# Third convolution: nine-tap products in f32r with stacked high and low parts, weights split in the stage

## The reference, cut to what matters

```python
def _L2_conv_ref(x, w_qkv, head_scale, w_out, gamma, beta):   # x comes in as _ln_c(x)
    ...
    qkv = lax.conv_general_dilated(x, w_qkv, (1, 1), 'SAME', ...)   # 3x3, 64 -> 384 channels
    q, k, v = jnp.split(qkv, 3, axis=1)                             # 8 heads of 16 each
    attn = jnp.einsum('bgnd,bgmd->bgnm', q, k)
    qn = jnp.sqrt(jnp.sum(q * q, axis=-1) + SMOOTH)
    kn = jnp.sqrt(jnp.sum(k * k, axis=-1) + SMOOTH)
    attn = attn / (qn[:, :, :, None] * kn[:, :, None, :] + SMOOTH)
    s = jax.nn.sigmoid(head_scale) * (0.4 - 0.003) + 0.003
    pb = jnp.exp(-(1.0 / (2.0 * s * s))[:, None, None] * dis[None, :, :])
    pb = pb / jnp.sum(pb, axis=-1, keepdims=True)
    out = jnp.einsum('bgnm,bgmd->bgnd', attn * pb[None], v)
    ...
```

## Time and profile before

| | us |
|---|---|
| median of 3 runs | 771.08 (768.73 to 773.09) |
| the profiled execution, its device time | 772.89 |
| its span, first to last instruction | 771.1 |
| the stage touched, first load to `sums(0)` of the attention | 358.70 to 411.42 |
| matmuls of line 1334 within it | 72 records, 36 in the program |

### The profile page before, as it was taken

How to read it: one execution, slowest core, us unless ns; L and a number is a source line. 1 busy time by engine, 2 the same in 40 slices (tenths; PEclk the granted TensorE clock), 3 DMA queues, 4 the chain that set the end, 5 groups by cost and what they waited for, 6 DMA issues and landing times. The chain is left out here.

```text
span 771.1 us, 8274 instructions
## 1 busy us (share of the span) xinstructions
PE 589.8 (76%) x2469; PEld 353.7 (46%) x2469; DVE 501.7 (65%) x1226; ACT 377.9 (49%) x568; POOL 278.0 (36%) x219
## 2 busy tenths in 40 slices
PE   4663879999995698482997775599875997988781
PEld 2563657777773484261444442433533534751110
DVE  2772566777775653666954654882287893849986
ACT  3002647888873740252536652364023245939852
POOL 4998357788784100301005760500012382000000
PEclk9997689999997799576998557599579798569995
DMA  3441000000000500402000000300021000000000
GB/s 107 114 119 45 1 1 1 0 1 1 0 2 13 101 0 1 154 1 79 7 1 0 1 1 1 84 1 0 1 64 28 0 2 8 1 0 0 0 0 14
DMA packets 18516, 18.44 MB, mean 24 GB/s; under 512 B 10954, under 2 KB 14347, under 8 KB 18088
## 3 DMA queue, kind: packets, MB, share of 16 engines
q1 hardware_dynamic: 18472, 17.93, 8.9%
HBM read 17.02 MB, written 0.26 MB: 22 GB/s over the span
## 5 line engine op out<-in xcount | busy, mean ns | idle before, releaser
L646 POOL TENSOR_TENSOR l0f_hid_lo<-l0f_hid,l0f_hid_hi 114x512 fp32r<-114x512 f32 (+1 forms) x75 | 98.0, 1317 | 48.6 <-ACT l0f_hid_hi L728 47.8
L824 DVE TENSOR_TENSOR l0f_hid<-l0f_silu,PS 114x512 f32<-114x512 f32 x96 | 65.7, 687 | 41.8 <-ACT l0f_silu L745 40.7
L682 PE MATMUL PS<-l0f_xs,l0w_hi 128*114 128x512 f32 x192 | 78.6, 409 | 0.0
L682 PE MATMUL PS<-l0f_xs,l0w_lo 128*114 128x512 f32 x192 | 77.5, 403 | 0.0
L745 ACT ACTIVATE l0f_silu<-PS 114x512 f32<-114x512 f32 x96 | 57.7, 602 | 31.9 <-PE PS L682 31.2
L2530 PE MATMUL PS<-l3f_ring,l3f_slots 128*32 128x512 f32 x128 | 54.9, 647 | 13.0 <-DVE l3f_ring L2611 13.0
L728 ACT CAST l0f_hid_hi<-l0f_hid 114x512 fp32r<-114x512 f32 x96 | 59.1, 615 | 2.9 <-DVE l0f_hid L824 2.3
L1325 POOL TENSOR_TENSOR l2c_den<-l2c_far,l2c_den 128x1024 f32<-128x1024 f32 x16 | 37.6, 2358 | 63.2 <-ACT l2c_den L1483 63.2
L2611 DVE SCALAR_TENSOR_TENSOR l3f_ring<-l3f_ring,l_countT 128x1024 f32<-128x1024 f32 x32 | 39.0, 1226 | 10.4 <-ACT l3f_ring L2561 10.4
L2557 ACT ACTIVATE l3f_ring<-l3r_plain,l3r_neg 128x1024 f32<-128x1024 f32 x32 | 36.0, 1134 | 11.9 <-PE PS L2530 11.9
L2605 DVE SCALAR_TENSOR_TENSOR l3f_ring<-l3f_slope,l3r_low,l3f_ring 128x1024 f32<-128x1024 f32 x32 | 40.9, 1285 | 0.4 <-ACT l3f_ring L2557 0.4
(11 more groups left out here) (581 smaller groups left out, 1327.2 us busy)
## 6 DMA issues: line engine op xcount, KB each, us to landing
l0w_raw<-in_l_w SPq DMA_DIRECT2D x32, 170.5 KB, 3.2
l3k_edge<-in_edges SPq DMA_DIRECT2D x2, 1024.0 KB
l2c_wqkv<-in_l_wqkv SPq DMA_DIRECT2D x3, 384.0 KB, 4.3
l0w_w<-in_l_w SPq DMA_DIRECT2D x8, 142.5 KB
l2f_raw<-in_l_w SPq DMA_DIRECT2D x2, 512.0 KB, 6.2
l1c_pos_w<-in_l_pos_w SPq DMA_DIRECT2D x1, 784.0 KB, 4.7
l1c_vrow<-l1c_vimg SPq DMA_DIRECT2D x7, 88.0 KB, 4.0
l1f_raw<-in_l_w SPq DMA_DIRECT2D x2, 256.0 KB
```

The costliest lines, as they stand in the source:

```text
L646: g.tensor_tensor(hid_lo[0:k, q % HIDS, :], hid[0:k, q % HIDS, :], hid_hi[0:k, q % HIDS, :], ALU.subtract).then_inc(S("low_pool"), 1)
L682: last = t.matmul(m.PS[0:k, (one, two)[z], :], half[:, e, z, a:a + k], xs[:, h * HALF:(h + 1) * HALF], start=(half is ew.hi), stop=(half i ...
L824: v.tensor_tensor(hid[0:k, at % HIDS, :], silu[0:k, at % RING0, :], m.PS[0:k, two, :], ALU.mult).then_inc(S("free"), 1)
```

## The change

Images and weights are split into a high part, rounded to f32r, and a low part, the rest, also f32r. `xp` keeps its two halves, but they now hold the high part of the image (partitions 0 to 63, written by ACT) and the low part (64 to 127, DVE: bank of PSUM minus high part). The nine taps are no longer paired. One product for two images is 9 matmuls with 128 rows (high weights, standing in both halves, on both parts of the images) and 9 with 64 rows (low weights on the high part of the images), all f32r with 512 columns.

The weights come in f32 by 18 loads (6 per product: two copies of three rows of taps) of 64 partitions each, into `raw`, which lies in the tile `den`. ACT rounds them into `hi` (3 times 128 x 1152), and POOL subtracts into `lo` (3 times 64 x 1152), which lie in tiles that are used later. `xp` is zeroed by a POOL copy of a zeroed tile instead of a memset, since it is f32r. The copy of the transposed input to `XT` is left out. `q2` now shares the tile of `k2`.

```diff
         def _(sp):
             for z in (1, 0, 2):
-                sp.dma_start(wqkv[:, :, z, :], w["l2_wqkv"][:, :, z, :]).then_inc(S(f"w_conv{z}"), 16)
+                for half in range(2):
+                    for dy in range(3):
+                        src = w["l2_wqkv"][(dy % 2) * C:(dy % 2 + 1) * C, 3 * (dy // 2):3 * (dy // 2) + 3, z, :]
+                        sp.dma_start(raw[half * C:(half + 1) * C, z, 3 * dy:3 * dy + 3, :], src).then_inc(S(f"w_conv{z}"), 16)
             for dst, src in ((hs, "l2_hs"), (dis, "dis"), (parity, "parity")):
                 sp.dma_start(dst[:], w[src]).then_inc(S("w_first"), 16)
...
         @block.gpsimd
         def _(g_):
-            g_.memset(xp[:], 0.0).then_inc(m.sem("padded_zero"), 1)
+            g_.memset(blank[:], 0.0).then_inc(S("blank"), 1)
+            g_.wait_ge(S("blank"), 1)
+            g_.tensor_copy(xp[:].rearrange("p b h w -> p (b h w)"), blank[:, 0:1].broadcast_to([P, B * PADH * PADW])).then_inc(m.sem("padded_zero"), 1)
             g_.wait_ge(m.sem("padded_zero"), m.pads + 1)
             g_.memset(vt[:], 0.0).then_inc(S("vt_zero"), 1)
             g_.wait_ge(S("vt_zero"), 1)
+            for j, z in enumerate((1, 0, 2)):
+                g_.wait_ge(S("high"), j + 1)
+                g_.tensor_tensor(lo[z], raw[0:C, z], hi[0:C, z], ALU.subtract).then_inc(S("low"), 1)
...
             def conv(z, h, bank):
 
-                for j, (dy, dx) in enumerate(PAIRS):
-                    last = t.matmul(m.PS[:, bank, :], wqkv[:, j, z, :], xp[:, 2 * h:2 * h + 2, dy:dy + HH, dx:dx + WW],
-                                    start=(j == 0), stop=(j == len(PAIRS) - 1))
+                images = slice(2 * h, 2 * h + 2)
+                for j, (dy, dx) in enumerate(TAPS):
+                    t.matmul(m.PS[:, bank, :], hi[:, z, j, :], xp[:, images, dy:dy + HH, dx:dx + WW], start=(j == 0), stop=False)
+                t.wait_ge(S("low"), 1 + (1, 0, 2).index(z))
+                for j, (dy, dx) in enumerate(TAPS):
+                    last = t.matmul(m.PS[:, bank, :], lo[z][:, j, :], xp[0:C, images, dy:dy + HH, dx:dx + WW], start=False, stop=(j == len(TAPS) - 1))
...
         @block.scalar
         def _(a):
-            images_scalar(a, m, xp)
+            k = m.norms + 1
+            a.wait_ge(m.sem("norm_var"), k)
+            a.activation(m.stat[:, 2, :], m.stat[:, 1, :], ACT.Sqrt).then_inc(m.sem("norm_dev"), 1)
+
+            def round_high(z):
+                a.wait_ge(S(f"w_conv{z}"), 96)
+                a.copy(hi[:, z], raw[:, z]).then_inc(S("high"), 1)
+
+            a.wait_ge(m.sem("padded_zero"), m.pads + 1)
+            for b in range(B):
+                if b % 2 == 0:
+                    a.wait_ge(m.sem("norm_turned"), 2 * (k - 1) + b // 2 + 1)
+                a.copy(xp[0:C, b, 1:1 + HH, 1:1 + WW], turned(b)).then_inc(S("image_high"), 1)
+                if b == 1:
+                    round_high(1)
+            a.copy(m.XT[0:1, 0:1], m.ident[0:1, 0:1]).then_inc(m.sem("norm_xt"), 2)
+            round_high(0)
+            round_high(2)
             a.wait_ge(S("w_first"), 48)
             a.activation(hs[:], hs[:], ACT.Exp, scale=-1.0).then_inc(S("minus_exp"), 1)
...
-            images_vector(v, m, xp)
+            v.wait_ge(m.sem("padded_zero"), m.pads + 1)
+            for b in range(B):
+                v.wait_ge(S("image_high"), 2 * (b // 2) + 2)
+                v.tensor_tensor(xp[C:2 * C, b, 1:1 + HH, 1:1 + WW], turned(b), xp[0:C, b, 1:1 + HH, 1:1 + WW], ALU.subtract).then_inc(S("image_low"), 1)
```

27 lines of the change are left out of this document (17 added, 10 removed).

## The result

The changed kernel took 781.06 us in the median of 4 runs (778.91 to 781.37), the kernel before 770.05 in 4 runs beside it (768.73 to 773.09). The ratio is 1.013, with a 95% interval of 1.009 to 1.017: slower by 11 us. The forecast was 775.9, and the range ended at 780.5.

A forecast was written before the change was run, and what follows sets the result against it. In the third convolution TensorE ran without a hole, with a second chain (ACT, VectorE) 0.2 us behind. norm_rows(1) 7.9 us late, minus 3.1 from three products, gives +4.8: 772.89 + 4.8 - 1.81 = 775.9 us, range 771.3 to 780.5.

The forecast's parts named there:

- The delay of the chain: Third convolution: late loads, roundings and a POOL subtraction delay the exponential and first step on hs, hence pb, by 7.7 us.
- D: Lateness of the chain from hs through pb to the z sums and rz: 7.7 us, ends 6.5 and 8.6.
- The z sums: TensorE's z sums, behind idle time of 7 us or so, start at half clock and take 6.8 us instead of 4.5.
- The first product on the path: conv(0, 0), ahead of norm_rows(1): a product costs 4.1 us, and norm_rows(1) starts 7.9 us late.
- The gain of three products: Between norm_rows(1) and sums(0), three cheaper products give back 3 x 1.02 = 3.1 us.
- windows slow the stream: Rival: f32r matmuls on padded windows take 0.43 us (790) or 0.29 (780.0) instead of 0.23; chance 0.08.
- Bytes as the bound of the loads: Rival: bytes at 268 GB/s, not issue, pace the 18 loads; D 3.3 to 5.9, time 771.3 to 773.9; chance 0.2.
- A low clock through all of the z sums and beyond: Rival: TensorE's clock stays low past the z sums; its price is cut from the text, half lies outside the range.
- own range: 774.5 to 777.4 us, for D from 6.5 to 8.6 and the clock back after 3 to 6 us.
- the wide one: 771.3 to 780.5 us, from the low end of the byte-bound case to the smaller window case.

The follow-up runs named there:

- hs_first_fit: hs_first with POOL's subtraction for q moved behind the z sums and that for v behind VectorE's first split: 775.10 us, 3.7 above the kernel before.
- three_loads: The changed kernel with the weights laid out on the host and loaded by three 128-row loads instead of eighteen of 64 rows: 779.9 us.
- hs_first: The changed kernel with hs, dis and parity loaded behind the first six weight loads and the exponential of hs ahead of the second and third rounding: 779.4 us.
- combo: The changed kernel with three 128-row loads, sign loads and exponential moved ahead, and low weights of 128 rows: 776.58 us, 1.006 of the kernel before.
- combo_late: combo with POOL's second and third subtraction moved behind VectorE's eight far products: 778.0 us, 1.008 of the kernel before.
- late_hs: The kernel before with 15 idle 64-row loads put ahead of the loads of hs, dis and parity, products still paired f32: 1.010 of the kernel before.
- lo128: The changed kernel with low weights of 128 rows and no wait for them in the second product of each kind: 1.007 of the kernel before.
- fit: combo with POOL's subtraction for q moved behind the z sums and that for v behind VectorE's first split: 771.19 us against 771.43, ratio 1.0001.
- after: The changed kernel itself, as profiled: median 781.06 us, 1.013 of the kernel before.
- forms: The changed kernel with other operand forms in the q and v products and no low-weight wait in each second product; results not right, no time given.
- three_late: three_loads with POOL's second and third subtraction moved behind VectorE's eight far products: 781.3 us, 1.012 of the kernel before.
- combo64: combo with low weights of 64 rows again; no time given, sums(0) starts 3.6 us later than in combo.

## Why the prediction came out as it did

The direction and the mechanism were right: the loads are paced by SP, the roundings wait for them, the exponential waits for the roundings, POOL's third subtraction holds the first VectorE step, and the z sums start late and at half clock. The size was too small: +4.8 forecast for `sums(0)`, +10.1 measured there, and 11 in the time.

**The delay of the chain.** Forecast D = 7.7, measured 8.2 (17.65 - 9.44), within its ends. The loads went every 0.66 us instead of 0.61, which is 0.8 us over 17 of them (the prediction's own had this pace: three loads of 128 rows in 1.99 us, so the number of rows does not tell the pace, as it had taken); the shorter landing of 2.5 gave 0.4 back. The hold by POOL was as forecast: the step ended 0.04 us behind the subtraction.

**The z sums.** Forecast 6.8 us at half clock and back, measured 6.5; `norm_rows(0)` started at rel. 32.9, forecast 32.7. The k products were forecast to end by rel. 19.3 and ended near 22.7, since the clock stayed low for 12.7 us and not 3 to 6. So TensorE idled for 3.6 us ahead of the z sums where 7 or so were forecast. The later end cost nothing here, for `pb` was later still; in hs_first_fit, where `pb` ended at 20.65, the same late clock kept the z sums back until 22.67.

**The first product on the path.** Forecast `norm_rows(1)` at rel. 38.5, measured 39.6. conv(0, 0) took 5.3 us from its start to the next group's where 4.1 was forecast; the start of `norm_rows(0)`, 0.2 later than forecast, and the row sums' 0.3 less (1.4 instead of 1.7) make it 1.1. With the delay of the chain it makes `norm_rows(1)` late by 9.0.

**The gain of three products.** This is the step that failed most. The sum had 3 x 1.02 = 3.1 us back between `norm_rows(1)` and `sums(0)`; that way took 23.16 us instead of 22.07, so 1.1 was lost and the miss is 4.2. Where it went (the first three points make 2.5, the last 1.7):

- The value 0.23 for an f32r matmul on a window was wrong: it is 0.257. Over 18 matmuls that is 0.5 us a product. The rival "windows slow the stream" had the right mechanism and its smaller size, 0.29, was too high.
- The change of rows between the halves was in no part of the prediction, which so put it at nothing: 0.3 us a product.
- What is left is 0.19 of the forecast 1.02: row sums and product, from `norm_rows(3)` to `sums(0)`, took 6.96 before and 6.77 after. With 128 rows it is 6.46. Three times the missing 0.83 makes 2.5 of the 4.2.
- The clock fell for 3.4 us behind the wait of TensorE for ACT: `norm_rows(2)` to `norm_rows(3)` took 8.45 us, 1.7 above the 6.77 of its like. The prediction had the clock as a question of the z sums alone.

1.1 + 2.5 + 1.7 = 5.3, the difference of 10.1 and 4.8.

**The rivals.** Bytes as the bound of the loads is refuted by three_loads: the same bytes came at up to 422 GB/s, and the last rounding ended 4.7 us earlier. The 268 GB/s that priced this rival was no ceiling either. A low clock through all of the z sums and beyond did not occur: it came back at 30.6, ahead of `norm_rows(0)` at 32.9. The forecast's own range (774.5 to 777.4) and the wide one (to 780.5) both ended below the median: they took in a dearer window or a low clock, each alone, and a part of both came, with the change of rows on top.

**What the prediction did not see** is how much POOL can cost. It priced the subtractions once, where they held one step, and in the changed kernel that was all, 1.1 us. But with the chain repaired the second and third of them cost 5 us: `rz` starts at 32.9 in hs_first, combo and combo_late, and at 27.94 in the two kernels with the subtractions moved. The wait for the late loads had hidden it. Costs measured one by one (7.7 in late_hs, 2.9 in lo128, 5.0 from combo to fit) therefore add up to more than the 10.1 lost.

**What stays open.** Whether the 64-row matmuls or something that goes with them moves the clock is not shown. Five kernels with all f32r matmuls of 128 rows, whose clock had last risen 20.6 to 20.8 us ahead of the stage's first load, got it back at 13.4 to 13.6; five with 64 rows whose clock had last risen 20.5 to 20.6 us ahead (after, forms, three_loads, three_late, hs_first_fit) at 20.3 to 20.5. Where the last rise lay at -22, two kernels with 64 rows (hs_first, combo64) had it at 12.0 and 11.7, no later than late_hs, whose products are f32 (11.9). In the kernel before, with f32 products and the last rise at -20.5, it came at 10.2. A fall between the z sums and `sums(0)` came in six of the seven kernels with 64 rows (all but hs_first_fit), and with 128 rows in combo_late alone, where TensorE had waited for 6 us. So the rows may be a cause, but only one profile of each kernel stands behind this, and since the point of the last rise differs by itself from run to run, a single profile can mislead by some microseconds.

## What to carry to other kernels

When work is handed to GpSimd, look up which VectorE instructions stand beside it, not how long they are: one of 0.17 us on SBUF lasts as long as GpSimd's instruction, and a chain of tiny ones meets several. Put such work beside instructions that were seen not to be held (here MAX8, and a TENSOR_TENSOR with one operand in PSUM), or in VectorE's idle time; with orders alone changed, this kernel lost 3.7 us instead of 11.

A cheaper product is worth what its neighbours leave of it: price it by the distance between starts in the form in which it will run, window, rows and the f32 work around it included. And load in few large transfers: eighteen small ones held back the exponential they had nothing to do with.
